# Five sums of weights by transfers that add, issued by GpSimd, in place of VectorE

## The chip, the cores and the metric

One core of one Trainium2 chip runs the kernel. The metric is the device time of one execution in microseconds (us), the median of three runs. The core's engines are PE (TensorE, matrix products), DVE (VectorE), ACT (ScalarE), POOL (GpSimd) and SP (SyncE, which here only issues transfers); 16 DMA engines move the data. Each engine works through its own queue in order, and semaphores order the engines against each other.

## What is computed

For 64 items x of 128 x 1024 there are two stages, each with its residual:

```python
w = weights[conditions]                      # one 128 x 128 matrix per item
x = x + einsum('bct,bcd->bdt', x, w)
H = einsum('btd,od->bto', x, W)              # W is 1024 x 1024, the same for all items
xa = einsum('btd,brd->btr', x, A[adapter_idx])
delta = einsum('btr,bor->bto', xa, Bm[adapter_idx]) * s_b
x = x + H + delta
```

## The kernel before

The kernel moves the second stage ahead of the first: x is multiplied by W plus the identity and by the low-rank adapter, and then the result z by the item's condition matrix plus the identity. Items go in pairs, 32 steps in all. W is cut in 4 x 3 blocks b00 to b32 of 256 rows by 342 columns (a tile of 128 partitions x 2 x 342 numbers, 342 KB). The pair's x is cut in the same manner, and a fast scheme for block products needs, for a pair, 20 products of sums of x blocks with sums of W blocks in place of 24 plain ones. The sums of W are the same for all steps, so they are made once, during step 0.

Step 0 (function `dense`, L1541 to L1557) runs plain 32-bit products on the raw blocks as they arrive from memory. Step 1 (`whole_product`) runs 32-bit products on the sums of W. All later steps (`product`, L1377) run on sums that are split in a high part (ACT, `hi_of`, into `w_hi`) and a rest (DVE, `rest_of`, into `w_lo`). Products and sums share their numbers: the sum "2" is the weight of product 2, and it stands in the slot `slot("lo", "2")` of `w_lo_raw`; an intermediate sum has a letter or an "a" ("f", "12a"). The names "hi" and "lo" of a slot only say in which of two raw tiles it lies.

What sets the order in the first 45 us is written out by hand, a list for each engine:

- SP (L386 to L413): loads x and the 12 blocks of W, then x of step 1, then waits for the split of the adapter matrices B (`z_hi[0]` and `z_lo[0]`, used here as scratch) and stores both parts to the table `b_split` in DRAM (`save_b`), loads the adapter A of step 1, the condition matrices of step 0, waits for both stores (`b_saved` at 32, L412) and loads from that table the rows of step 0 (`load_b`) into `b_stack_raw`.
- POOL (L467 to L505): adds the identity to six blocks of W as they arrive, writes the scaled adapter columns of step 0 (`first_rides`), and after the last block, b22 (L494), picks the scalings of step 1 and makes its adapter columns (`make_rides`, L276 to L299), and writes them beside the sums (L501 and L502, `whole_rides_ready`), which PE needs at product 5 of step 1.
- DVE (L1174 to L1263): the sums, in the order of the blocks' arrival (`DVE_SUMS` lists it; `made` waits for a sum by its place in that list), the sums of x for step 1, the adapter's first product of step 0, then `rest_c` (L1234, the rest of the condition matrices, which waits for ACT's `hi_of_c`), and behind it the last sums: 3, 6, 12a, 12, 1a and 1, and the rests of z.
- ACT (L740 to L834): the high parts in the order 17, 13, 5, 15, then the high part of B, then 2, 0, 4, 14, 18, 10, 7 and 11 (L756 to L772), then `hi_of_c`, the two `turned_xa` (which write `g_sb`), and `take_b` (L776), which makes `b_stack`.
- PE (L1560 to L1596): `dense` of the 12 blocks; ahead of the last, b22, stand the two turns of the adapter's first product and the three products `lora("10")`, `lora("11")`, `lora("12")`, which wait for `g_sb` and for `b_stack` (`b_ready`, L1587). Then step 1 begins with product 17, the adapter products of item 0, products 5 and 15 and a part of the condition product of step 0, then 13 and 2.

## Time and profile before

| | us |
|---|---|
| median of three runs | 772.71 |
| lowest and highest of the three | 772.51, 773.09 |
| the profiled execution | 773.48 |
| its span in the profile | 771.7 |
| PE busy in it | 760.3 (99%) |
| DVE, ACT and POOL busy | 613.8, 503.9, 190.1 |

In the profile, the start is where engines wait for blocks of W, and from 75 us on the steps repeat. The timeline of an engine lists its instructions in order of time, with equal ones merged: the start, the length of the whole group, the count (x3), and in brackets how long the engine had been idle before and what it waited for. PE's records of a 32-bit product count two for each of the kernel's matmuls. A transfer shows on its issuing engine's queue (SPq) only with the time that the issue took; its landing is in the view of its tile.

### The profile page before, as it was taken

To read this page: it belongs to the slowest core of one execution; us is meant where nothing else is said; L and a number is where in the kernel's file an instruction comes from. 1 tells how busy PE (TensorE), PEld (TensorE's weight loads), DVE (VectorE), ACT (ScalarE), POOL (GpSimd) and SP (SyncE) were. 2 spreads that over 40 slices of the span, in tenths; PEclk is the share of its full clock that TensorE was granted. 3 is DMA by queue.
4 is the path that set the end of the run, shared out by engine and by line. 5 is a ranking of instruction groups with operands and counts; after the bars stand their busy time and mean duration, and the time that the engine had idled before them with its cause. 6 is when DMAs were issued, how large, how long until landed. Compare 5 with 4: busy or idle time off the path is not lost.

```text
span 771.7 us, 16748 instructions
## 1 busy us (share of the span) xinstructions
PE 760.3 (99%) x4418; PEld 719.3 (93%) x4418; DVE 613.8 (80%) x1386; ACT 503.9 (65%) x1173; POOL 190.1 (25%) x428
## 2 busy tenths in 40 slices
PE   7999999999999999999999999999999999999998
PEld 4567999999999999999999999999999999999997
DVE  5999977788777788777788777788777788777774
ACT  3476666676666676666676666676666676666673
POOL 2733202233212333202332212323212232212200
PEclk9999999999999999999999999999999999999999
DMA  8433343432343432333432343432343432343222
GB/s 288 169 131 116 124 144 123 151 120 90 122 143 122 150 117 94 122 143 122 150 118 92 122 143 122 150 112 98 122 143 122 150 117 94 122 143 122 89 90 83
DMA packets 47291, 98.32 MB, mean 127 GB/s; under 512 B 6438, under 2 KB 25894, under 8 KB 47270
## 3 DMA queue, kind: packets, MB, share of 16 engines
q1 hardware_dynamic: 47266, 98.08, 37.4%
q8 instruction: 9, 0.15, 0.1%
q14 instruction: 12, 0.10, 0.0%
q10 hardware_dynamic: 4, 0.00, 0.0%
HBM read 63.45 MB, written 34.60 MB: 127 GB/s over the span
## 4 chain that ended last, share of the span: by engine, by line
PE 87%; DVE 3%; DMA 1%; issue 1%; ACT 0%; SPq 0%; DVEq 0%; ACTq 0%
PE bank L1381 73%; PE o_ps L1442 4%; PE bank L1420 3%; PE o_ps L1441 3%; PE o_ps L1443 3%; DMA out<-o_sb 1%; DVE c_sb L892 1%; DVE w_lo L889 1%; DVE z_lo L889 0%; DVE x_lo L889 0%; PE bank L1425 0%; PE o_ps L1432 0%; DVE x_raw L889 0%; ACT x_hi L510 0%; ACT z_hi L510 0%
## 5 line engine op out<-in xcount | busy, mean ns | idle before, releaser
L1381 PE MATMUL bank<-w_hi,x_hi 128*128 128x342 f32 (+2 forms) x1200 | 390.5, 325 | 0.7 <-ACT c_sb L510 0.6
L1381 PE MATMUL bank<-w_lo,x_hi 128*128 128x342 f32 (+2 forms) x1200 | 387.1, 323 | 0.0
L1381 PE MATMUL bank<-w_hi,x_lo 128*128 128x342 f32 (+2 forms) x1200 | 386.5, 322 | 0.0
L1381 PEld LDWEIGHTS bank<-w_hi,x_hi 128*128 128x128 f32 x1200 | 225.8, 188 | 9.8 <-ACT c_sb L510 2.1
L1381 PEld LDWEIGHTS bank<-w_lo,x_hi 128*128 128x128 f32 x1200 | 225.6, 188 | 2.8
L1381 PEld LDWEIGHTS bank<-w_hi,x_lo 128*128 128x128 f32 x1200 | 226.1, 188 | 0.0
L889 DVE TENSOR_TENSOR x_lo<-x_raw,x_hi 128x256 fp32r<-128x256 f32 (+1 forms) x270 | 145.5, 547 | 32.0 <-ACT x_hi L510 27.3
L510 ACT ACTIVATE x_hi<-x_raw 128x256 fp32r<-128x256 f32 (+1 forms) x270 | 133.7, 507 | 52.5 <-PE bank L1381 45.7
L303 POOL TENSOR_TENSOR w_lo<-a_ride,w_hi 128x160 fp32r<-128x160 f32 x30 | 15.6, 519 | 507.0 <-ACT w_hi L510 507.0
L510 ACT ACTIVATE c_sb<-bank 128x342 f32<-128x342 f32 x190 | 85.7, 452 | 41.0 <-PE bank L1381 38.6
L510 ACT ACTIVATE z_hi<-c_sb 128x340 fp32r<-128x340 f32 (+1 forms) x128 | 60.4, 490 | 54.8 <-DVE c_sb L892 54.8
L892 DVE TENSOR_TENSOR c_sb<-bank,c_sb 128x342 f32<-128x342 f32 x186 | 91.1, 504 | 3.6 <-PE bank L1420 2.5
L510 ACT ACTIVATE o_sb<-o_ps 128x512 f32<-128x512 f32 x124 | 73.9, 596 | 14.3 <-PE o_ps L1443 12.6
L889 DVE TENSOR_TENSOR x_lo<-t_sb,x_hi 128x512 fp32r<-128x512 f32 x60 | 41.5, 692 | 36.2 <-ACT x_hi L510 36.2
L889 DVE TENSOR_TENSOR z_lo<-c_sb,z_hi 128x340 fp32r<-128x340 f32 (+1 forms) x128 | 69.4, 544 | 0.4 <-ACT z_hi L510 0.2
L889 DVE TENSOR_TENSOR xa_sum<-bank,c_sb 128x16 f32<-128x16 f32 x31 | 5.4, 174 | 62.7 <-PE bank L1381 62.7
L510 ACT ACTIVATE bank<-bank 128x342 f32<-128x342 f32 (+1 forms) x93 | 41.3, 444 | 15.8 <-PE bank L1381 15.3
L1441 PE MATMUL o_ps<-z_hi,c_hi 128*128 128x512 f32 x126 | 50.5, 401 | 0.0
L1442 PE MATMUL o_ps<-z_lo,c_hi 128*128 128x512 f32 x126 | 49.8, 396 | 0.0
L1443 PE MATMUL o_ps<-z_hi,c_lo 128*128 128x512 f32 x126 | 49.5, 393 | 0.0
L279 POOL TENSOR_TENSOR a_ride<-a_now,s_now 128x32 f32<-128x32 f32 x93 | 43.7, 496 | 16.8 <-DMA a_now<-lora_a 10.1
L1420 PE MATMUL bank<-b_stack,g_sb 128*128 128x340 f32 (+1 forms) x192 | 46.4, 324 | 0.5 <-ACT b_stack L510 0.5
(104 smaller groups left out, 878.2 us busy)
## 6 DMA issues: line engine op xcount, KB each, us to landing
x_raw<-xT SPq DMA_DIRECT2D x62, 512.0 KB, 4.9
out<-o_sb SPq DMA_DIRECT2D x62, 512.0 KB, 2.7
b_stack_raw<-b_split SPq DMA_DIRECT2D x128, 128.0 KB, 2.4
a_now<-lora_a SPq DMA_DIRECT2D x64, 64.0 KB, 3.4
c_raw<-cond_w SPq DMA_DIRECT2D x64, 64.0 KB, 1.8
w_lo_raw<-wB SPq DMA_DIRECT2D x7, 342.0 KB, 7.5
w_hi_raw<-wB SPq DMA_DIRECT2D x5, 342.0 KB, 6.0
x_raw<-xT SPq DMA_DIRECT2D x4, 256.0 KB, 4.7
```

The costliest lines, as they stand in the source:

```text
L279: unit.tensor_tensor(to, a_now[:, n, k:k + count, :], s_now[:, n:n + 1].unsqueeze(2).to_broadcast([P, count, 2 * R]), ALU.mult).then_inc(a ...
L303: unit.tensor_tensor(left_rides(w_lo), rides(0, 5), left_rides(w_hi), ALU.subtract).then_inc(ride_ready, 1)
L510: return nc.scalar.activation(to, x, ACT.Copy)
L889: return nc.vector.tensor_tensor(to, x, y, ALU.subtract)
L892: return nc.vector.tensor_tensor(to, x, y, ALU.add)
L1381: last = nc.tensor.matmul(bank[:, lo:hi], x[:, left, c * C:(c + 1) * C], w[:, c, FIRST[o]:FIRST[o] + WIDTH[o]], start=opens and c == 0 and ...
L1420: nc.tensor.matmul(main_of(bank_of(j, d, role), cols.stop - cols.start), g_sb[n][:, :], b_stack[:, cols], start=False, stop=True, skip_gro ...
L1441: nc.tensor.matmul(bank[:, :], c_hi[:, n, :], z_hi[n][:, cols], start=True, stop=False)
L1442: nc.tensor.matmul(bank[:, :], c_hi[:, n, :], z_lo[n][:, cols], start=False, stop=False)
L1443: nc.tensor.matmul(bank[:, :], c_lo[:, n, :], z_hi[n][:, cols], start=False, stop=True)\
```

## The change

Five sums leave DVE's list: 2, 18, 11, 12 and 1. Each is now one transfer that POOL issues, which adds a block to what its destination holds (`add_on`, with `accum_op`). Before each but the first, POOL waits until the one before has landed (`dma_summed`, 16 for each). The destinations of 2 and 18 are first filled by SP with the blocks b30 and b31, loaded from DRAM a second time, between the loads of x for step 1 and the stores of B; POOL waits for both (`first_parts_landed`). The other three already stand in their slots: "11a" in slot 11, "12a" in block b31's slot and "1a" in b02's. The adds of 2 and 18 stand in POOL's list behind the identity of b22, the one of 11 behind the pick of the scalings and ahead of `make_rides`, the ones of 12 and 1 behind the copies of L501 and L502. `made` waits for `dma_summed` where a reader names one of the five; ACT's list of high parts stays in its order. DVE waits for "f" now ahead of sum 14. Some semaphores are merged (`ident_zero` into `ident_ready`, `ones_ready` and `zeros_ready` into `filled`), which changes no wait's meaning.

```diff
@@ -55,8 +55,10 @@
     DENSE = ("b12", "b01", "b21", "b30", "b20", "b10", "b00", "b11", "b31", "b02", "b32", "b22")
     SPLITS = ("17", "13", "5", "15", "2", "0", "4", "14", "18", "10", "7", "11", "9", "8", "16", "1", "3", "19", "6", "12")
     POOL_SUMS = ("i21a", "i21b", "i10", "i11a", "i11b", "i00", "i32", "i22")
-    DVE_SUMS = ("s", "5", "v", "e", "f", "0", "2", "7", "18", "4", "y", "11a", "14", "10", "11", "3", "6", "12a", "12",
-                "1a", "1", "9", "16a", "16", "19a", "19")
+    DVE_SUMS = ("s", "5", "v", "e", "f", "0", "7", "4", "y", "11a", "14", "10", "3", "6", "12a", "1a", "9", "16a", "16",
+                "19a", "19")
+
+    DMA_SUMS = ("2", "18", "11", "12", "1")

     WHOLE_SUMS = ("u_0", "u12", "v", "u_1", "u", "u910", "u67", "u11", "u54", "u3")

...
@@ -263,6 +265,9 @@
                 eng.wait_ge(pool_summed, max(on_pool))
             if on_dve:
                 eng.wait_ge(dve_summed, max(on_dve))
+            on_dma = [DMA_SUMS.index(n) + 1 for n in names if n in DMA_SUMS]
+            if on_dma:
+                eng.wait_ge(dma_summed, max(on_dma) * 16)

         def left_rides(w):
             return w[:, :, 0:5 * EDGE].rearrange("p c (o q) -> p o c q", q=EDGE)[:, :, :, 0:R]
@@ -401,6 +406,8 @@
             sp.dma_start(cond_sb[:, :], cond_idx).then_inc(cond_landed, 16)
             load_x(0, 0, 1, 0)
             load_x(0, 0, 1, 1)
+            for o, b in (("2", "b30"), ("18", "b31")):
+                sp.dma_start(slot("lo", o), wB[int(b[1]), int(b[2]), :, :, :]).then_inc(first_parts_landed, 16)
             sp.wait_ge(b_hi_ready, 1)
             save_b(0, z_hi[0])
             sp.wait_ge(b_lo_ready, 1)
@@ -464,11 +471,17 @@
                 nc.gpsimd.tensor_tensor(where, where, ident[:, :].unsqueeze(1).to_broadcast([P, 2, P]), ALU.add)\
                     .then_inc(pool_summed, 1)

-            nc.gpsimd.memset(ident[:, :], 0.0).then_inc(ident_zero, 1)
-            pool.wait_ge(ident_zero, 1)
+            def add_on(name, to, x):
+
+                if DMA_SUMS.index(name):
+                    pool.wait_ge(dma_summed, DMA_SUMS.index(name) * 16)
+                nc.gpsimd.dma_start(to, x, accum_op=ALU.add).then_inc(dma_summed, 16)
+
+            nc.gpsimd.memset(ident[:, :], 0.0).then_inc(ident_ready, 1)
+            pool.wait_ge(ident_ready, 1)
             nc.gpsimd.affine_select(out=ident[:, :], in_=ident[:, :], compare_op=ALU.not_equal, fill=1.0,
                                     base=0, pattern=[[-1, P]], channel_multiplier=1).then_inc(ident_ready, 1)
-            pool.wait_ge(ident_ready, 1)
+            pool.wait_ge(ident_ready, 2)
             pool.wait_ge(adapter_landed, 16)
             pool.wait_ge(s_tab_ready, 1)
             pick_scalings(0, 0, 0)
@@ -492,14 +505,24 @@
             add_identities("b32", 84)
             pool.wait_ge(w_landed["b22"], 16)
             add_identity("b22", 1, 0, 44, 84)
+            pool.wait_ge(first_parts_landed, 32)
+            made(pool, "f")
+            add_on("2", slot("lo", "2"), slot("hi", "12"))
+            add_on("18", slot("lo", "18"), slot("hi", "12"))
             pool.wait_ge(first_scaled, 8)
             pick_scalings(0, 0, 1)
+            made(pool, "11a", "e")
+            add_on("11", slot("lo", "11"), slot("hi", "6"))
             make_rides(pool, nc.gpsimd, 0, 0, 1)

             dense_through(pool, "b10")
             pool.wait_ge(a_summed, 4)
             nc.gpsimd.tensor_copy(left_rides(w_lo_raw), rides(0, 5)).then_inc(whole_rides_ready, 1)
             nc.gpsimd.tensor_copy(right_rides(w_lo_raw), rides(5, 4)).then_inc(whole_rides_ready, 1)
+            made(pool, "12a", "s")
+            add_on("12", w_block("b31"), slot("hi", "19"))
+            made(pool, "1a", "i00")
+            add_on("1", w_block("b02"), w_block("b00"))
             pool.wait_ge(whole_rides_ready, 2)
             step(0, 1)
             run_steps(pool, step)
...
@@ -814,7 +837,7 @@
             made(act, "19", "11")
             in_place("6")
             hi_a1(0, 1, 1)
-            made(act, "19a", "14", "18")
+            made(act, "19a", "14", "18", "2")
             in_place("12")
             begin_c02(0, 1)
             turned_xa(0, 1, 0, 1)
@@ -1171,10 +1194,10 @@
             def summed(name):
                 dve.wait_ge(whole_summed, WHOLE_SUMS.index(name) + 1)

-            nc.vector.memset(ones[:, :], 1.0).then_inc(ones_ready, 1)
-            nc.vector.memset(xa_cols[0][:, :], 0.0).then_inc(zeros_ready, 1)
-            nc.vector.memset(xa_cols[1][:, :], 0.0).then_inc(zeros_ready, 1)
-            dve.wait_ge(ident_ready, 1)
+            nc.vector.memset(ones[:, :], 1.0).then_inc(filled, 1)
+            nc.vector.memset(xa_cols[0][:, :], 0.0).then_inc(filled, 1)
+            nc.vector.memset(xa_cols[1][:, :], 0.0).then_inc(filled, 1)
+            dve.wait_ge(ident_ready, 2)
             nc.vector.tensor_copy(ident_r[:, :], ident[:, :]).then_inc(ident_r_ready, 1)
             rest_of("17", w_block("b12"))
             dve.wait_ge(w_landed["b01"], 16)
@@ -1190,14 +1213,10 @@
             add("f", slot("hi", "12"), w_block("b21"), slot("hi", "19"), ALU.subtract)
             made(dve, "e")
             add("0", slot("lo", "0"), slot("hi", "6"), slot("hi", "19"), ALU.subtract)
-            made(dve, "f")
-            add("2", slot("lo", "2"), slot("hi", "12"), w_block("b30"), ALU.add)
             dve.wait_ge(b_hi_ready, 1)
             subtract(z_lo[0][:, :], b_raw[:, :], z_hi[0][:, :]).then_inc(b_lo_ready, 1)
             made(dve, "i10")
             add("7", slot("lo", "7"), w_block("b10"), w_block("b12"), ALU.subtract)
-            dve.wait_ge(w_landed["b31"], 16)
-            add("18", slot("lo", "18"), slot("hi", "12"), w_block("b31"), ALU.add)
             made(dve, "i11b")
             add("4", slot("lo", "4"), w_block("b11"), w_block("b12"), ALU.subtract)
             dve.wait_ge(w_landed["b02"], 16)
@@ -1205,6 +1224,7 @@
             made(dve, "i00")
             add("11a", slot("lo", "11"), w_block("b00"), w_block("b12"), ALU.subtract)
             made(dve, "i32")
+            made(dve, "f")
             add("14", slot("lo", "14"), slot("hi", "12"), w_block("b32"), ALU.add)
             dve.wait_ge(x_landed[1][0], 16)
             dve.wait_ge(x_landed[1][1], 16)
@@ -1217,8 +1237,6 @@
             add("10", slot("lo", "10"), slot("hi", "6"), slot("lo", "8"), ALU.subtract)
             summed("u_1")
             whole("u", subtract, x_whole[:, U, :], x_whole[:, U, :], raw(0, 1)[:, 0, 2, :])
-            made(dve, "11a")
-            add("11", slot("lo", "11"), slot("lo", "11"), slot("hi", "6"), ALU.add)
             summed("u")
             whole("u910", plus, x_whole[:, U9:U, :], twice(x_whole[:, U, :]), x_whole[:, U1:U6, :])
             whole("u67", subtract, x_whole[:, U6:U5, :], twice(raw(0, 1)[:, 0, 2, :]), x_whole[:, U1:U6, :])
@@ -1239,12 +1257,8 @@
             add("6", w_block("b11"), w_block("b11"), w_block("b01"), ALU.subtract)
             dense_through(dve, "b31")
             add("12a", w_block("b31"), w_block("b31"), w_block("b32"), ALU.subtract)
-            made(dve, "12a")
-            add("12", w_block("b31"), w_block("b31"), slot("hi", "19"), ALU.add)
             dense_through(dve, "b02")
             add("1a", w_block("b02"), slot("lo", "8"), w_block("b30"), ALU.subtract)
-            made(dve, "1a")
-            add("1", w_block("b02"), w_block("b02"), w_block("b00"), ALU.add)
             rest_z("10", 0, 0, 0)
             rest_z("11", 0, 0, 0)
             dve.wait_ge(product_done["17"], 1)
...
```

## Rows read from the trace of the kernel before

**Rows 1.** The page's busy times: engine, us (share of the span), instructions.

```profile
PE 760.3 (99%) x4418; PEld 719.3 (93%) x4418; DVE 613.8 (80%) x1386; ACT 503.9 (65%) x1173; POOL 190.1 (25%) x428
```

**Rows 2.** Windows: stretch, length, busy times by engine, granted clock, DMA share, GB/s.

```profile
17.00:22.50 5.50, 4.74 (x16) 2.76 (x15) 4.29 (x4) 2.05 (x3) 4.83 (x7) 1.00 1.06 395
22.50:27.50 5.00, 4.71 (x16) 2.77 (x15) 4.38 (x9) 2.21 (x3) 3.80 (x6) 1.00 0.60 237
...
250.00:500.00 250.00, 250.00 (x1515) 244.21 (x1514) 199.29 (x464) 170.01 (x402) 62.77 (x143) 1.00 0.38 127
```

**Rows 3.** Timeline of PE, 0 to 75 us: start, length, what, idle before.

```profile
20.68 2.67 PE L1553 MATMUL bank<-w_lo_raw,x_raw 128*128 128x358 f32 x8 [0.76 <-POOL w_lo_raw L451]
23.64 2.67 PE L1553 MATMUL bank<-w_hi_raw,x_raw 128*128 128x358 f32 x8 [0.29 <-POOL w_hi_raw L451]
...
36.21 0.71 PE L1420 MATMUL bank<-b_stack,g_sb 128*128 128x342 f32 x3 [0.47 <-ACT b_stack L510]
...
40.67 2.52 PE L1397 MATMUL bank<-w_lo_raw,x_whole 128*128 128x358 f32 x8
42.77 0.65 PE L1441 MATMUL o_ps<-z_hi,c_hi 128*128 128x512 f32 x1
...
70.04 0.43 PE L1381 MATMUL bank<-w_hi,x_hi 128*128 128x342 f32 x1 [0.63 <-ACT c_sb L510]
```

**Rows 4.** Timeline of ACT, 0 to 75 us.

```profile
17.63 1.42 ACT L510 ACTIVATE w_hi<-w_lo_raw 128x684 fp32r<-128x684 f32 x2
...
28.34 2.10 ACT L510 ACTIVATE w_hi<-w_lo_raw 128x684 fp32r<-128x684 f32 x3 [0.95 <-DVE w_lo_raw L1152]
31.77 0.42 ACT L510 ACTIVATE c_hi<-c_raw 128x256 fp32r<-128x256 f32 x1 [1.33 <-DVE c_raw L892]
33.31 0.28 ACT L510 ACTIVATE g_sb<-o_ps 128x128 fp32r<-128x128 f32 x1 [1.13 <-PE o_ps L1432]
...
35.01 1.06 ACT L510 ACTIVATE b_stack<-b_stack_raw 128x1024 fp32r<-128x1024 f32 x1 [1.25 <-DMA b_stack_raw<-b_split]
```

**Rows 5.** Timeline of SP, 0 to 75 us; its lengths are those of the issues.

```profile
15.74 0.84 SPq L318 DMA_DIRECT2D x_raw<-xT  x2
17.75 0.74 SPq L378 DMA_DIRECT2D b_split<-z_hi  x1
...
30.92 2.16 SPq L338 DMA_DIRECT2D b_stack_raw<-b_split  x4
```

**Rows 6.** Waits of SP's queue, 0 to 80 us: total, times, longest.

```profile
SPq L323 <- DMA b_split<-z_lo: 1.2, 1, 1.2
```

**Rows 7.** Timeline of POOL, 0 to 75 us.

```profile
24.86 0.33 POOL L457 TENSOR_TENSOR w_lo_raw<-w_lo_raw,ident 128x84 f32<-128x84 f32 x1
...
30.19 1.26 POOL L279 TENSOR_TENSOR a_ride<-a_now,s_now 128x32 f32<-128x32 f32 x3 [3.90 <-DMA a_now<-lora_a]
...
36.14 0.93 POOL L502 COPY w_lo_raw<-a_ride 128x128 f32<-128x128 f32 x1
```

**Rows 8.** Views of the tiles w_lo_raw (342 KB) and c_raw (64 KB): issue to landing.

```profile
DMA to landing us min/median/max: 4.3/7.5/8.0
...
DMA to landing us min/median/max: 1.7/2.0/2.4
```

**Rows 9.** Timeline of DVE, 0 to 75 us.

```profile
14.83 1.64 DVE L1152 TENSOR_TENSOR w_lo_raw<-w_hi_raw 128x684 f32<-128x684 f32 x2
...
32.41 0.56 DVE L889 TENSOR_TENSOR c_lo<-c_raw,c_hi 128x256 fp32r<-128x256 f32 x1
...
36.05 2.65 DVE L1152 TENSOR_TENSOR w_lo_raw<-w_lo_raw,w_hi_raw 128x684 f32<-128x684 f32 x3
...
40.41 0.87 DVE L1152 TENSOR_TENSOR w_lo_raw<-w_lo_raw 128x684 f32<-128x684 f32 x1 [0.86 <-PE bank L1397]
```

**Rows 10.** Groups of PE by shape, 4 to 12 us: count, busy us, mean ns, idle.

```profile
L1553 PE MATMUL bank<-w_lo_raw,x_raw 128*128 128x342 f32 x8 | 4.9, 795 | 1.6 <-DMA w_lo_raw<-wB 1.6
L1553 PE MATMUL bank<-w_hi_raw,x_raw 128*128 128x342 f32 x6 | 1.9, 454 | 0.0
```

More of the change, by code:

```diff
@@ L128, in cond_resid_kernel @@
         x_half_landed = [sem(f"x_half_landed{n}") for n in range(2)]
-        ones_ready = sem("ones_ready")
+        filled = sem("filled")
         s_spread = sem("s_spread")
@@ L140, in cond_resid_kernel @@
         table_loaded = sem("table_loaded")
-        ident_zero = sem("ident_zero")
         ident_ready = sem("ident_ready")
         ident_r_ready = sem("ident_r_ready")
-        zeros_ready = sem("zeros_ready")
         pool_summed = sem("pool_summed")
         dve_summed = sem("dve_summed")
+        dma_summed = sem("dma_summed")
+        first_parts_landed = sem("first_parts_landed")
         w_hi_ready = sem("w_hi_ready")
@@ L741, in _ @@
             act.dma_start(s_row[:, :], scalings).then_inc(s_landed, 16)
-            act.wait_ge(ident_ready, 1)
+            act.wait_ge(ident_ready, 2)
             copy(table[0:32, 0:1], ident[0:32, 0:1]).then_inc(table_loaded, 1)
@@ L1560, in _ @@
             pe.wait_ge(s_landed, 16)
-            pe.wait_ge(ones_ready, 1)
+            pe.wait_ge(filled, 1)
             nc.tensor.matmul(o_ps[0][:, 0:NAD], ones[0:1, :], s_row[0:1, :], start=True, stop=True).then_inc(s_spread, 1)
```

## The prediction

> **What bounds the kernel now.** I read the page first. PE is busy in 760.3 of 771.7 us and DVE in 80% [rows 1]; between 250 and 500 us PE is busy for all of the 250.00 [rows 2]. Nothing that this change touches runs there, and what PE loses in the first 75 us is not given back later: PE has no gap in which to catch up. The question is only by how much the change moves PE's start-up.
>
> The second view was PE's timeline of that start. After its first block PE waits four times: 0.76 and 0.29 us for columns that POOL writes, 0.47 us at 36.21 for `b_stack`, the first operand of the adapter products, and 0.63 us at 70.04 for a copy by ACT [rows 3]. Together that is 2.15 us, the most that any relief of DVE could bring. None of the four names DVE. DVE even ends its list of sums early: it waits 0.86 us for PE ahead of 40.41 [rows 9].
>
> The third view was the list of ACT, because the adapter products at 36.21 wait for two things that ACT makes: `g_sb` (33.31) and `b_stack` (35.01) [rows 4]. ACT's list is in order, and the high parts of 2, 18 and 11 stand in it ahead of both. The fourth was SP's queue: `b_stack` waits for transfers that SP issues from 30.92 on, after a wait for the store of B [rows 5, 6].
>
> **What it removes.** Five DVE instructions of about 0.88 us (three in 2.65 us) [rows 9], 4.4 us. The adds of 2 and 18 stood where DVE waited for blocks and for POOL anyway. The one of 11 stood ahead of `first_split`, which leads to `g_sb`, but PE reaches the turn behind its own dense products, and after it `b_stack` is what is late, by its transfer [rows 3, 4]. The ones of 12 and 1 stood just before the 0.86 us wait for PE [rows 9]; a wait takes their place. Value of the removal: 0, at most 2.15 us as above.
>
> **The two added loads.** SP issues two more transfers between the loads of x, whose issue ends at 16.58 (15.74 + 0.84), and the store of the high part of B at 17.75, for which it had been waiting [rows 5]. At about 0.6 us each (0.84 us for two of x is the nearest row) they fill that gap; the issue costs nothing. Their data does cost. From 17 to 22.5 us the DMA engines are full (share 1.06, 395 GB/s), and then run at 237 GB/s with a share of 0.60 until 27.5 [rows 2]; I read the first as the loads and the second as mostly the two stores of B, which stand behind the loads in SP's queue. Two blocks of 342 KB are 0.70 MB; at 395 GB/s that is 1.8 us, by which the stores end later. SP waits for them (1.2 us of wait in before, so there is no slack [rows 6]), issues the loads of B 1.8 us later, and `b_stack` starts at 36.8 in place of 35.01, PE's adapter products at 38.0 in place of 36.21. That alone is +1.8 us. It would be 0 if the loads fitted beside the stores in the 40% that those leave idle, and more if POOL's adds, which fall in the same stretch, take share from the stores; I take 1.8, with bounds 0 and 2.8.
>
> **The three adds ahead of the adapter products.** POOL ends the identity of b22 at 25.2 (24.86 + 0.33) [rows 7]. The filled slots of 2 and 18 end with the loads at about 24.3 (22.5 + 1.8), and with the time that a small transfer takes to report I put the start of the first add at 25.7. Then the three adds run one behind the other, since POOL waits for each landing before it issues the next. The trace has no transfer by POOL, none that adds, and none between two tiles of SBUF. The nearest rows: 64 KB in an idle queue take 1.7 us at least, 342 KB in a full queue take 4.3 to 8.0 us [rows 8]. These are my two ends, 1.7 and 8.0 for each add. I take 4.3: same size, a queue only half full, but one that has to read the destination as well as the source. So 2 lands at 30.0, 18 at 34.3 and 11 at 38.6.
>
> ACT waits for 2 at about 17.6, where it started on it in before [rows 4]. At 30.0 it does 2, 0, 4 and 14, at 34.3 it does 18, 10 and 7, and at 38.6 it does 11. Behind it are 0.70 us for the high part (2.10 for three), 0.42 for `c_hi`, two times 0.28 for `g_sb` and 1.06 for `b_stack` [rows 4], 2.7 us in all and 2.6 with their overlap. The B rows have landed by then (36.8). PE's adapter products start at 41.2 in place of 36.21, **+5.0 us**. The 1.8 us of the loads are inside this, not on top: the later of the two sets the start.
>
> What is queued behind these waits. On ACT: the condition matrices' high part, `g_sb`, `b_stack` and all the copies of z. On DVE: `rest_c` waits for ACT's `c_hi`, so DVE stands from about 31 to 39.2, and the sums 3, 6, 12a and 1a and the rests of z come after it. In before `c_lo` ran 3.8 us ahead of the adapter products (32.41) [rows 9], now 2.0 ahead; but two adds of 0.88 us are gone behind it, so the rests of z end as far ahead of the condition products (42.77 in before [rows 3]) as they did. On POOL: `make_rides` starts behind the issue of add 11, about 35.3 (1 us for the issue, above the 0.6 of SP) in place of 30.19, takes the same 6.9 us until its copies end (37.07 in before [rows 7]), and is done at 42.3; PE needs it at 40.67 + 5.0 = 45.7 [rows 3]. The add of 12 then waits for 12a (about 43.3), lands at 47.6, the one of 1 at 51.9; ACT needs it about 57. Those two I cost at 0; their cover is 5 us.
>
> **The sum.** The profiled execution took 773.5 us against a median of 772.7; the sum made on it is carried to the median as a difference. 772.7 + 5.0 = 777.7.
>
> A rule of the skill against this length. The Trainium skill, "DMA: Bandwidth & Descriptors", section "Anatomy of one DMA", gives a transfer issued by GpSimd about 2.0 us plus its bytes at 436 GB/s, which would be an estimate of 2.8 us for each add; no row here shows such a transfer. By that the third add would land at 34.1, ACT would be through at 36.7, and the loads (38.0) would set the start: the time of the first rival below, not mine.
>
> **The rivals.**
> *Short adds.* Below 3.3 us each, the third lands before 35.6 and ACT is through before 38.2; then the late `b_stack` sets the start, +1.8 to +2.8 us, 774.5 to 775.5. For it: the DMA engines are nearly idle from 28 us on. Against: each add is a chain of issue, read, read, write and report, and the smallest 342 KB row is 4.3 us. 0.16.
>
> *The chain, and a slow clock after it.* PE idles 0.47 + 5.0 us in one stretch. At the start of the kernel, after such idle time, eight 32-bit matmuls took 795 ns each, while later ones of the same shape took 454 [rows 10]: the shorter is that of 2.4 GHz, the longer nearer 1.2 GHz, though the granted clock in the windows reads 1.00. If PE falls back, the next eight cost (795 - 454) x 8, 2.7 us as busy times overlap little, about 2.3 from their starts: 777.7 + 2.3 = 780.0. The Trainium skill, "TensorE: Matmul & The Clock Gate" (section "HAM oscillation"), says that waits between bursts of matmuls put the clock back to half; here no wait of such length shows between PE's first block and the end. 0.20.
>
> *Long adds.* Above 5.3 us each (a destination read that halves the rate, or an issue on POOL of over 1 us), +8 to +16 us, 780.7 to 789. 0.08.
>
> *Not slower.* DVE's relief decides, and the adds are hidden: if they land by 33 us (2.4 us each) and the two loads fit beside the stores, ACT is never late. Then DVE's 4.4 us can take away the 0.63 us at 70.04 and some of POOL's 0.76 and 0.29, where POOL works beside DVE: 772.7 - 0.6 = 772.1, at the most 770.6. Against: both conditions at once, and DVE's wait of 0.86 us for PE swallows what it saves. 0.06. That the transfers do not replace the DVE work is excluded by the lists.
>
> **How the numbers follow.** The forecast, adds of 3.3 to 5.3 us, +2.0 to +8.0, 774.7 to 780.7: 0.50. The range has to leave out no more than 0.2: 774.3 to 782.5 leaves out most of the long adds, the not-slower case and the tail of the clock case. A difference of about 0.2% (1.5 us) is what a measurement of this kernel can tell from none. Faster by more: 0.02. Within: 0.06 (the rest of the not-slower case, and the low edge of the short adds). Slower: 0.92.
>
> **What would show it.** In the profile of the changed kernel: the first `w_hi` copy after `z_hi` on ACT at 30 and the one of 11 at 38.6, POOL as what ACT waited for, or a DMA; the adapter products of PE at 41.2 with an idle time of about 5.5 us named `b_stack` or `g_sb`; `b_stack_raw` loaded by 36.8; DVE with a gap of some 7 us ahead of `c_lo`; from 75 us on the same steps. The prediction is wrong if ACT reaches `c_hi` before 35, if PE waits anywhere else for over 1 us, or if the span outside the first 75 us changes.

## The result, and the profile after

The changed kernel takes 785.05 us (median of four runs, 784.82 to 785.59), the kernel before, run beside it, 772.87 us: a ratio of 1.0155, 95% interval 1.0143 to 1.0168. It is slower by 12.2 us. The prediction said 777.7 us, 774.3 to 782.5. Its sign holds, and so does the path it named (adds one after another, ACT's list behind them, PE last); its size does not, and a second cost, PE's slow clock, was missing from its sum.

| | before | after |
|---|---|---|
| profiled execution, us | 773.48 | 785.16 |
| span in the profile, us | 771.7 | 783.3 |
| PE starts the adapter products of step 0 | 36.21 | 45.01 |
| PE starts product 5 of step 1 | 40.67 | 52.33 |
| PE busy, 250 to 500 us | 250.00 | 250.00 |

The lines on the span and on product 5 close the sum: product 5 starts 11.66 us late, and the span is 11.6 us longer, so the loss is complete by 53 us. (The medians differ by 12.2 us and the two profiled executions by 11.7: the profiled one of before lies 0.6 us above its median.)

The page's line of busy times (engine, us, share of the span, instructions), which answers [rows 1]. PE's work has grown by 2.3 us though it does the same 4418 instructions; DVE has five fewer, POOL five more.

```profile
PE 762.6 (97%) x4418; PEld 721.1 (92%) x4418; DVE 609.1 (78%) x1381; ACT 503.7 (64%) x1173; POOL 194.2 (25%) x433
```

PE's largest wait (engine, line, what it waited for: us in total, times, longest). In before this wait was 0.47 us.

```profile
PE bank L1434 <- ACT b_stack L533: 9.7, 1, 9.7
```

PE's timeline around it (start, length, what, count, idle before), which answers [rows 3].

```profile
32.79 2.51 PE L1567 MATMUL bank<-w_lo_raw,x_raw 128*128 128x342 f32 x8
45.01 1.19 PE L1434 MATMUL bank<-b_stack,g_sb 128*128 128x342 f32 x3 [9.70 <-ACT b_stack L533]
46.00 4.76 PE L1567 MATMUL bank<-w_lo_raw,x_raw 128*128 128x342 f32 x8
50.55 1.47 PE L1411 MATMUL bank<-w_lo_raw,x_whole 128*128 128x342 f32 x4
51.60 0.89 PE L1434 MATMUL bank<-b_stack,g_sb 128*128 128x342 f32 x3
52.33 2.52 PE L1411 MATMUL bank<-w_lo_raw,x_whole 128*128 128x358 f32 x8
```

Read two things here. The wait ends 8.80 us later than in before (45.01 against 36.21). And behind it eight matmuls of one shape take 4.76 us, where the same eight took 2.51 us before the wait, at 32.79. From the adapter products to product 5 there are 7.32 us, in before 4.46 (40.67 - 36.21). That is 2.86 us more for the same work: 8.80 + 2.86 = 11.66.

The windows say what that is (stretch, length, busy times of PE, PEld, DVE, ACT, POOL with counts, granted clock, DMA share, GB/s). The clock is at 0.50, which is the level of 1.2 GHz, from 42 us on, and goes back to full within the window from 50 on.

```profile
40.00:42.00 2.00, 0.00 (x0) 0.00 (x0) 0.00 (x0) 0.00 (x0) 1.77 (x7) 0.65 1.08 175
42.00:44.00 2.00, 0.00 (x0) 0.00 (x0) 0.38 (x2) 1.49 (x5) 0.59 (x3) 0.50 0.01 4
...
45.00:50.50 5.50, 5.49 (x11) 3.69 (x12) 3.35 (x6) 1.55 (x4) 1.20 (x1) 0.50 0.39 58
...
50.00:55.00 5.00, 5.00 (x19) 3.49 (x18) 2.94 (x6) 3.39 (x9) 2.02 (x3) 0.91 0.79 259
250.00:500.00 250.00, 250.00 (x1515) 244.24 (x1515) 199.07 (x464) 168.85 (x400) 59.48 (x136) 1.00 0.38 125
```

Why the wait is so long is in ACT's list, which answers [rows 4].

```profile
33.09 2.76 ACT L533 ACTIVATE w_hi<-w_lo_raw 128x684 fp32r<-128x684 f32 x4 [15.86 <-DMA w_lo_raw<-w_hi_raw]
37.74 2.10 ACT L533 ACTIVATE w_hi<-w_lo_raw 128x684 fp32r<-128x684 f32 x3 [1.89 <-DMA w_lo_raw<-w_hi_raw]
42.51 0.77 ACT L533 ACTIVATE w_hi<-w_lo_raw 128x684 fp32r<-128x684 f32 x1 [2.67 <-issue]
43.19 0.40 ACT L533 ACTIVATE c_hi<-c_raw 128x256 fp32r<-128x256 f32 x1
43.49 0.26 ACT L533 ACTIVATE g_sb<-o_ps 128x128 fp32r<-128x128 f32 x1
43.65 0.27 ACT L533 ACTIVATE g_sb<-bank 128x128 fp32r<-128x128 f32 x1
43.81 1.05 ACT L533 ACTIVATE b_stack<-b_stack_raw 128x1024 fp32r<-128x1024 f32 x1
```

The three groups start at the landings of 2, 18 and 11, and behind the last stands the tail to `b_stack`. The wait of 15.86 us is for the first add. The 2.67 us ahead of the third group are labelled "issue", since the profile didn't pair them with a transfer, but POOL's list does (second column is the issue alone, it answers [rows 7]):

```profile
26.36 1.33 POOL L478 DMA_DIRECT2D w_lo_raw<-w_hi_raw  x1 [2.30 <-DMA w_lo_raw<-wB]
33.37 1.20 POOL L478 DMA_DIRECT2D w_lo_raw<-w_hi_raw  x1 [5.67 <-DMA w_lo_raw<-w_hi_raw]
...
38.24 1.19 POOL L478 DMA_DIRECT2D w_lo_raw<-w_hi_raw  x1 [3.38 <-DMA w_lo_raw<-w_hi_raw]
...
47.02 1.20 POOL L478 DMA_DIRECT2D w_lo_raw<-w_hi_raw  x1 [3.93 <-DVE w_lo_raw L1175]
52.98 1.19 POOL L478 DMA_DIRECT2D w_lo_raw<-w_hi_raw  x1 [4.76 <-DVE w_lo_raw L1175]
```

The second and the third follow on the landing of the one before; the first waited for SP's second loads of b30 and b31. The view of the tile w_lo_raw, from 24 to 45 us, has the time from issue to landing of these three: the first took 6.7 us, the third 4.2.

```profile
DMA to landing us min/median/max: 4.2/4.3/6.7
```

What ran beside the first is in SP's queue, whose line answers [rows 5]: SP issues the loads of `b_stack_raw` when both stores of B have landed, at 31.79, and in before at 30.92. So the stores were under way for most of the first add, and behind them in SP's list stand the small loads of the adapter and the condition matrices (24.79 and 27.20). From 26 to 31 us the DMA engines moved 243 GB/s at a share of 0.83, in before 125 GB/s at 0.37.

```profile
31.79 2.20 SPq L343 DMA_DIRECT2D b_stack_raw<-b_split  x4
```

### The profile page after: what moved, and what is told of

Its sections match the earlier page's. It is cut to its first block, busy times and chain, and to the rows that moved or that the text cites. A ratio compares the mean times of both kernels' runs of the same rounds, so it can differ in the third digit from the quotient of the medians.

```text
span 783.3 us, 16759 instructions
## 1 busy us (share of the span) xinstructions
PE 762.6 (97%) x4418; PEld 721.1 (92%) x4418; DVE 609.1 (78%) x1381; ACT 503.7 (64%) x1173; POOL 194.2 (25%) x433
## 3 DMA queue, kind: packets, MB, share of 16 engines
q0 software_dynamic: 1360, 1.75, 1.4%
## 4 chain that ended last, share of the span: by engine, by line
PE 86%; DVE 3%; DMA 1%; issue 1%; ACT 0%; SPq 0%; DVEq 0%; ACTq 0%
PE bank L1395 71%; PE o_ps L1456 3%; PE bank L1434 3%; PE o_ps L1455 3%; PE o_ps L1457 3%; DMA out<-o_sb 1%; DVE c_sb L915 1%; DVE w_lo L912 1%; DVE z_lo L912 0%; DVE x_lo L912 0%; PE bank L1439 0%; PE o_ps L1446 0%; DVE x_raw L912 0%; ACT x_hi L533 0%; ACT z_hi L533 0%
## 5 line engine op out<-in xcount | busy, mean ns | idle before, releaser
L533 ACT ACTIVATE c_sb<-bank 128x342 f32<-128x342 f32 x190 | 85.7, 451 | 43.8 <-PE bank L1395 38.6
```

Of the source, the lines that this page charges most:

```text
L533: return nc.scalar.activation(to, x, ACT.Copy)
```

## The experiments

The clock's cost is read everywhere in the same way: the time from the start of the adapter products to that of product 5 less the 4.46 us of before. I call it the second leg, and the start of the adapter products less 36.21 the first leg.

### Is DVE's relief worth anything, and do the late adds cost anything?

Only 12 and 1 are done by transfers, with the waits of the change; 2, 18 and 11 stay with DVE. Against the changed kernel:

```diff
-    DMA_SUMS = ("2", "18", "11", "12", "1")
+    DMA_SUMS = ("12", "1")
...
+            add("2", slot("lo", "2"), slot("hi", "12"), w_block("b30"), ALU.add)
...
```

> Only the sums 12 and 1 are added by transfers; 2, 18 and 11 stay with DVE and nothing is loaded twice. Theory of the ordered chain (only adds that stand ahead of ACT's operands of the adapter products cost anything): the same as before, 772.9 within 0.5 us, the adapter products at 36.2. Rival, that every such transfer costs in itself (POOL's time, traffic, DVE beside it): a fifth or more of the loss for each, 775 to 777.

Measured: 773.32 us, ratio 1.0002 (0.9992 to 1.0011), adapter products at 35.67, 0.5 us earlier than in the profiled execution of before (the blocks of W came earlier in this one, see the end). No difference that can be measured: two of the five transfers with DVE's relief by those two sums are worth nothing together.

### What do the two loads cost by themselves?

The kernel before, with two loads of the same size at the same place in SP's queue, into tiles that are idle there (`o_sb`, and `b_stack_raw`, whose later load waits for it).

```diff
+            for n, to, b in ((0, o_sb, "b30"), (1, b_stack_raw, "b31")):
+                sp.dma_start(to[:, 0:2 * N].rearrange("p (c q) -> p c q", q=N), wB[int(b[1]), int(b[2]), :, :, :])\
+                  .then_inc(extra_landed[n], 16)
             sp.wait_ge(b_hi_ready, 1)
             save_b(0, z_hi[0])
```

> The kernel before, and the two blocks are loaded a second time at the same place of SP's queue into tiles that are idle; no adds by transfers. By the step of the prediction the stores of B end 1.8 us later: 774.7. By the trace of the changed kernel, where SP issued the loads of B at 31.79 against 30.92: +0.9, 773.7. Rival, that the traffic made the loss: above 780.

Measured: 776.87 us, ratio 1.0043 (1.0029 to 1.0057). Its timeline of PE:

```profile
32.99 2.51 PE L1558 MATMUL bank<-w_lo_raw,x_raw 128*128 128x342 f32 x8
37.99 0.94 PE L1425 MATMUL bank<-b_stack,g_sb 128*128 128x342 f32 x3 [2.48 <-ACT b_stack L514]
38.73 3.94 PE L1558 MATMUL bank<-w_lo_raw,x_raw 128*128 128x342 f32 x8
```

The first leg is 1.78 us, as the prediction worked out (SP issues the loads of `b_stack_raw` at 32.40 in place of 30.92). The second leg, 1.68 us, was in no theory of this run: its window from 38 to 42 us has a granted clock of 0.57. A wait of 2.48 us was enough to lose the full clock. To show that the second leg is the clock and not something that the loads do, the next kernel adds four products of no use (into `o_ps[0]`, overwritten later) where PE would wait:

```diff
+            for n in range(4):
+                nc.tensor.matmul(o_ps[0][:, 0:N], x_raw[0][:, n % 2, 0, 0:C], w_block("b12")[:, n % 2, :],
+                                 start=True, stop=True)
```

> The kernel with the two added loads alone, and PE runs four idle products while it waits for b_stack. The start of the adapter products stays at 38.0. Theory of the slow clock: with the wait of 2.5 us nearly filled, the products after it keep 0.45 us each and 1.7 us come back, 775.1 against 776.9. Rival, that the extra comes from something else: 776.9.

Measured: 774.99 us (eleven runs), ratio 1.0024 (1.0015 to 1.0033). Its timeline of PE, in which L1592 is the filling:

```profile
35.48 2.46 PE L1592 MATMUL o_ps<-w_lo_raw,x_raw 128*128 128x342 f32 x8
37.83 0.71 PE L1425 MATMUL bank<-b_stack,g_sb 128*128 128x342 f32 x3
38.38 2.46 PE L1558 MATMUL bank<-w_lo_raw,x_raw 128*128 128x342 f32 x8
```

The adapter products start as late as without the filling, the matmuls behind them take 2.46 us again, and the kernel is 1.9 us faster. So the loads cost 1.7 to 1.8 us by delay (774.99 against 773.25 beside it, and the first leg), and 1.9 us by the clock that the delay loses.

### How much of the change is the clock?

The changed kernel with sixteen such products at the same place.

```diff
+            for n in range(16):
+                nc.tensor.matmul(o_ps[0][:, 0:N], x_raw[0][:, n % 2, 0, 0:C], w_block("b12")[:, n % 2, :],
+                                 start=True, stop=True)
```

> The changed kernel, and PE runs 16 idle products into a bank nobody reads while it waits for b_stack; nothing else is changed. Theory of the slow clock: the wait ends where it did (45.0), but the products after it take 0.45 us in place of 0.9, and 2.9 us come back: 782.2. Rival, that the slow products after the wait have another cause (operands that come late): 785.0, or more if the idle products outlast the wait.

Measured: 784.52 us, ratio 1.0145, but in two groups: 783.18 and 783.75, 785.30 and 786.21. The profile is of 785.30:

```profile
35.12 9.36 PE L1601 MATMUL o_ps<-w_lo_raw,x_raw 128*128 128x342 f32 x32
45.38 0.71 PE L1434 MATMUL bank<-b_stack,g_sb 128*128 128x342 f32 x3 [0.90 <-ACT b_stack L533]
45.93 2.46 PE L1567 MATMUL bank<-w_lo_raw,x_raw 128*128 128x342 f32 x8
...
49.86 2.52 PE L1411 MATMUL bank<-w_lo_raw,x_whole 128*128 128x358 f32 x8
...
101.87 0.30 PE L1439 MATMUL bank<-ident_r,xa_cols 128*128 128x128 f32 x1 [2.04 <-DVE xa_cols L912]
```

The second leg is gone (49.86 - 45.38 = 4.48). But at 101.87 PE waits 2.04 us, and the clock falls there (0.79 in the window from 100 to 108), so what was saved is lost again. ACT waits 3.08 us for the store of the outputs just before that, at 97.21. Since two of the four runs were 2.3 us faster, I ran the same kernel again to see one of the other group:

> The changed kernel with the 16 idle products once more, with more runs: four runs before lay at 783.2 to 786.2. Theory, that the filled wait keeps the clock, and that the clock can fall later, at another wait of about 2 us in step 3 (for the store of o_sb behind the loads of x): two groups of runs, at 782 to 784 where the mean clock is 1.0 and at 785 to 786 where it is 0.998 or less. Rival, that filling brings nothing: one group at 785.

Measured: 782.95, 782.74, 783.53 and 786.25. This time the profiled run is a fast one, 782.95: adapter products at 45.50, product 5 at 49.97, granted clock 1.00 in every window read, and no later wait of PE over 0.62 us. ACT waits 1.64 us for the same store here, and PE 0.59 us: each 1.4 us less than in the slow one, so PE's later wait goes back to that store. Against 785.05 that is 2.1 us, somewhat less than the 2.86 us of the second leg, in part because the adapter products start 0.5 us later. Why the store lands later in some runs of this kernel is open. Of these eight runs five lie at 782.7 to 783.8 us and three at 785.3 to 786.3.

### How long is an add, and why?

*Transport or the adding?* All five transfers copy in place of adding. The five sums then lack what their slots held, a part of each.

```diff
-                nc.gpsimd.dma_start(to, x, accum_op=ALU.add).then_inc(dma_summed, 16)
+                nc.gpsimd.dma_start(to, x).then_inc(dma_summed, 16)
```

> The changed kernel with the five transfers as plain copies: they overwrite the destination in place of adding to it, so the five sums lack one part. Bytes, order and waits are the same. Theory, that reading the destination and adding is a large part of the 4.6 us from issue to landing: 3.3 us each, the adapter products at about 41, 781. Rival, that a transfer issued by GpSimd takes as long in any case: 785.

Measured: 782.35 us, ratio 1.0111 (1.0095 to 1.0126), adapter products at 43.03. POOL's list, and the tile's view from 24 to 45 us:

```profile
26.37 0.88 POOL L478 DMA_DIRECT2D w_lo_raw<-w_hi_raw  x1 [2.37 <-DMA w_lo_raw<-wB]
32.49 0.73 POOL L478 DMA_DIRECT2D w_lo_raw<-w_hi_raw  x1 [5.24 <-DMA w_lo_raw<-w_hi_raw]
...
37.67 0.72 POOL L478 DMA_DIRECT2D w_lo_raw<-w_hi_raw  x1 [3.63 <-DMA w_lo_raw<-w_hi_raw]
...
DMA to landing us min/median/max: 2.8/4.6/5.8
```

The third alone, in its own window, is the 2.8. A copy of 342 KB takes 2.8 us with the DMA engines otherwise empty, the add in the same place 4.2 us, and its issue holds POOL for 1.20 us in place of 0.72. So adding costs 1.4 us in an empty queue. Only the third place compares like with like: the second copy took 4.6 us, no less than the second add (4.3), since SP issued the loads of `b_stack_raw` beside it at 32.60. The DMA queues of the first 80 us (packets, MB, share of the time of 16 engines), after first and then the copy, say where: more packets for the same sums, and twice the engines' time.

```profile
q0 software_dynamic: 1360, 1.75, 13.8%
...
q0 software_dynamic: 560, 1.75, 6.2%
```

*Does the first add pay for the stores of B?* SP stores B only after the add of 2 has landed; this takes the stores out of its way and puts them in that of the second. SP's list being in order, the small loads behind the stores move too, so that SP issues nothing beside the first add (from 17.67 to 31.07).

```diff
             sp.wait_ge(b_hi_ready, 1)
+            sp.wait_ge(dma_summed, 16)
             save_b(0, z_hi[0])
```

> The changed kernel, but SP stores B only after the add of 2 has landed, so nothing but the small loads runs beside that add. A look at one number: when the add that was issued at 26 lands. Theory, that its 7.1 us against 4.3 of the third came from the stores of B beside it: about 30.4, 4.4 us. Rival, that the first transfer of GpSimd's queue is slow in itself (its first issue took 1.33 us against 1.2): 33 again. The second add will be slower, beside the stores; the whole time is no measure here, 783 to 788.

Measured: 791.86 us, a single run. The first add is issued at 26.70 and takes 4.3 us to land, not the 6.7 of the change (the expectation's 7.1 is about the time to the next issue). The second, which now has the stores beside it, takes until 42.59, from 31.35:

```profile
31.07 2.76 ACT L534 ACTIVATE w_hi<-w_lo_raw 128x684 fp32r<-128x684 f32 x4 [13.52 <-DMA w_lo_raw<-w_hi_raw]
42.59 2.10 ACT L534 ACTIVATE w_hi<-w_lo_raw 128x684 fp32r<-128x684 f32 x3 [8.76 <-DMA w_lo_raw<-w_hi_raw]
```

So it isn't being the first in POOL's queue that makes an add slow. An add of this size costs 4.2 to 4.3 us with the DMA engines to itself, 6.7 us beside the end of the stores and the small loads, and 11.2 us beside the whole of the stores. How much of the 2.4 us between the first two is the stores' and how much the small loads' isn't shown.

*Does the chain of the three matter?* The three are issued one behind the other without a wait, and each reader waits for all of them. The last two lose their wait for each other in the same way.

```diff
-                if DMA_SUMS.index(name):
-                    pool.wait_ge(dma_summed, DMA_SUMS.index(name) * 16)
-                nc.gpsimd.dma_start(to, x, accum_op=ALU.add).then_inc(dma_summed, 16)
+                nc.gpsimd.dma_start(to, x, accum_op=ALU.add).then_inc(dma_summed[DMA_SUMS.index(name) > 2], 16)
```

> The changed kernel, but GpSimd issues the adds of 2, 18 and 11 without waiting for one another, on one semaphore, and readers wait until all three have landed; ACT's order is that of the changed kernel. Theory of the chain (each add is mostly latency: issue and report): all three land by about 35, ACT is through at about 43, and the adapter products start at 43 in place of 45, 782 to 783.5. Rival, that an add is mostly data (342 KB that take their 4 us of the DMA engines): the three land no earlier than 40, and then ACT does eight high parts behind them, 785 to 790.

Measured: 784.43 us, ratio 1.0145, above the 782 to 783.5 of the theory, and not by the rival's way either. All three land by 37.5 us (theory 35, rival 40 or later), 5.0 us before the third add of the change, yet PE gains 0.36 us. First the line of ACT:

```profile
37.52 5.41 ACT L529 ACTIVATE w_hi<-w_lo_raw 128x684 fp32r<-128x684 f32 x8 [20.56 <-DMA w_lo_raw<-w_hi_raw]
```

and that of PE:

```profile
44.65 1.19 PE L1430 MATMUL bank<-b_stack,g_sb 128*128 128x342 f32 x3 [9.62 <-ACT b_stack L529]
```

ACT now has all eight high parts still to do, 5.4 us, because the first of them waits for the last landing. In the change it does seven of them between the landings. The transport was shortened and ACT's own work took its place.

### Can it be mended?

*Order of ACT alone.* The high part of 2 moves behind the split of z, those of 18 and 11 behind the first seed of step 1, where their first readers are still far. Nothing that leads to `b_stack` waits for a transfer by POOL any more.

```diff
             hi_of("17", w_block("b12"))
...
-            made(act, "2")
-            in_place("2")
...
-            made(act, "18")
-            in_place("18")
...
-            made(act, "11", "e")
-            dense_through(act, "b20")
-            in_place("11")
...
+            made(act, "2")
+            in_place("2")
...
+            made(act, "18", "11", "e")
+            in_place("18")
+            in_place("11")
```

> The changed kernel with ACT's high parts of 2, 18 and 11 taken from ahead of the operands of the adapter products and put where ACT stands idle in step 1, before DVE needs them; all five transfers and both loads stay. Theory of ACT's order: b_stack is then late by its transfer alone, the adapter products start at about 37.2, 773.5 to 774.5. Rival, that the adds and loads themselves hold the start back: still above 778.

Measured: 779.24 us, ratio 1.0079 (1.0062 to 1.0096). It takes away 5.8 of the 12.2 us, less than expected. Its timeline of PE:

```profile
37.65 0.72 PE L1433 MATMUL bank<-b_stack,g_sb 128*128 128x342 f32 x3 [2.18 <-ACT b_stack L534]
38.21 4.15 PE L1566 MATMUL bank<-w_lo_raw,x_raw 128*128 128x342 f32 x8
...
59.29 1.42 PE L1410 MATMUL bank<-w_lo_raw,x_whole 128*128 128x342 f32 x4 [0.91 <-ACT c_sb L534]
```

and one line of ACT's:

```profile
57.46 1.44 ACT L534 ACTIVATE w_hi<-w_lo_raw 128x684 fp32r<-128x684 f32 x2 [3.05 <-DMA w_lo_raw<-w_hi_raw]
```

The first leg falls from 8.80 to 1.44 us with the five adds and both loads still in place, so ACT's order is what carries the adds to PE. The wait of 2.18 us still loses the clock (second leg 1.71 us). The rest, some 2 us, is new: the adds of 12 and 1, free in the first experiment, are late here. The one of 12, issued at 43.57 beside the loads of x (223 GB/s from 45 to 50 us), takes 7.8 us; POOL issues the one of 1 behind it, at 51.94, and ACT waits for that one until 57.46. This last reading rests on the trace of this kernel alone.

*All of it.* ACT's order is that of the last kernel, but with the high part of 2 still later (behind those of 9 and 8), the two loads stand behind the stores of B, and there is no chain, neither among the first three nor between the last two. The lines on the loads:

```diff
-            for o, b in (("2", "b30"), ("18", "b31")):
-                sp.dma_start(slot("lo", o), wB[int(b[1]), int(b[2]), :, :, :]).then_inc(first_parts_landed, 16)
             sp.wait_ge(b_hi_ready, 1)
             save_b(0, z_hi[0])
...
+            for o, b in (("2", "b30"), ("18", "b31")):
+                sp.dma_start(slot("lo", o), wB[int(b[1]), int(b[2]), :, :, :]).then_inc(first_parts_landed, 16)
```

> The five sums by transfers, with the three causes taken away: the second loads stand behind the stores of B, the adds of 2, 18 and 11 do not wait for one another, and ACT makes their high parts in step 1. If the three causes are all, the adapter products start at 36 to 37 and the time is that of before or up to 1.5 us above it, 773 to 774.5. Rival, that the adds' traffic beside the loads of B and of x holds something else back: 776 or more, with a wait on a transfer to show for it.

Measured: 774.98 us (ten runs, 773.05 to 778.31), ratio 1.0023 (1.0008 to 1.0038). Three runs with a mean granted clock of 0.998 took 777.0 to 777.2, six others 773.05 to 775.53. The profile is of one of the three: adapter products at 36.91 after 1.98 us of wait, product 5 at 43.07, a second leg of 1.70 us. In this kernel the clock falls in some runs and not in others; how long PE waited in the others isn't known, as only this one was profiled. With three products to fill the wait:

> The five sums by transfers with the three causes taken away, and PE runs three idle products in the 2 us that it still waits for b_stack. Theory, that the upper of its runs (777, mean clock 0.998) were the clock and the lower (773.1 to 774.4) the rest: all runs at 773.0 to 774.5, no group at 777. Rival, that the transfers' traffic spreads the times by itself: again up to 777 or more.

Measured: 773.93 us (eleven runs), ratio 1.0013 (1.0004 to 1.0022), ten of them between 773.57 and 774.70. In its timeline most of the loss is gone: a first leg of 0.26 and a second of 0.20 us.

```profile
36.47 0.90 PE L1429 MATMUL bank<-b_stack,g_sb 128*128 128x342 f32 x3
37.21 2.46 PE L1562 MATMUL bank<-w_lo_raw,x_raw 128*128 128x342 f32 x8
```

One run of each of the two kernels (778.31 and 776.82) was long at a full clock; I have no profile of either, and what they waited for is open. No version with the five transfers is faster than the kernel before.

## Why the prediction was wrong in size and right in kind

Two steps of it failed. It had the clock at nothing in the sum, and the clock cost 2.86 us. And it had each add at 4.3 us, where the first took 6.7 us, so that with smaller terms the third landed 3.9 us late.

- **What bounds the kernel.** Right. PE is again busy for the whole of 250 to 500 us, and all of the loss is ahead of product 5.
- **The removal, worth 0.** Nothing contradicts it. For 12 and 1 the first experiment measures removal and transfers together, and finds nothing. For 2, 18 and 11 no run has the removal without the cost; the nearest is the mended and filled kernel, which has all five removed and is not faster than before.
- **The two loads, 1.8 us by bytes over the measured rate.** Right to 0.1 us by itself: forecast 38.0, measured 37.99. What was missed is that this delay alone loses the clock, for another 1.7 to 1.9 us. So the "short adds" rival would not have given 774.5 to 775.5 but the 776.9 of the kernel with the loads alone.
- **The start of the first add.** Forecast 25.7, measured 26.36, as the two loads landed later than I had put them: +0.66 us.
- **The length of an add, 4.3 us each: the term that failed in the first leg.** Forecast landings 30.0, 34.3 and 38.6; measured 33.1, 37.7 and 42.5. For the second and third, with at most the small loads of `b_stack_raw` beside them, 4.3 was right (33.37 to 37.74 and 38.24 to 42.51). The first took 6.7, +2.4 us. I had read the DMA engines as half free from 22.5 to 27.5 [rows 2], and nearly idle from 28 on, and had not asked what stood there after the change, though my own step had moved the end of the stores back by 1.8 us. The kernel in which the stores wait gives 4.3 us for this same add, so the 2.4 us come from what SP's list has beside it: the stores, and the small loads behind them. Missing too was the step from one landing to the next issue, 0.28 us (33.09 to 33.37) and 0.50 us (37.74 to 38.24, behind the pick of the scalings). The sum is 0.66 + 2.4 + 0.28 + 0.50, but for rounding the 3.9 us by which the third landing is late.
- **ACT's tail, 2.6 us.** Right: 45.01 - 42.51 = 2.50. First leg forecast +5.0, measured +8.80: the 3.9 us less 0.1.
- **The clock: the term that was missing.** The mechanism stood as a rival with its price, 2.3 us; it measured 2.86 us. The price was for the eight matmuls behind the wait, and they took 2.25 us more from start to start (46.00 to 50.55, in before 36.76 to 39.06); left out were the adapter products themselves (0.44) and the matmuls behind the eight (0.17). The failure is in how the numbers followed: I made "the chain and a slow clock" exclusive of the forecast and gave it 0.20. The forecast itself had PE idle for 5.5 us, and the row from 4 to 12 us [rows 10] shows matmuls of 795 ns after idle time; behind the wait of the change the same shape took 777 ns, where the granted clock reads 0.50. Had the clock been a term of the sum, not a rival, the forecast would have been 780.0; with the adds at the upper end of that case (+8.0) 783.0. That is still 2 us short: the first leg of 8.80 lay just inside what I had kept for long adds. The Trainium skill, "TensorE: Matmul & The Clock Gate" (section "HAM oscillation"), states the fall to half when matmuls wait between bursts; the trace agrees, with 0.50 granted from 42 us on.
- **Long adds.** Of the three only the first was above the 5.3 us from which I counted an add as long, yet the sum passed that rival's +8. Long adds and a slow clock came together. By setting each against the forecast one by one I left their sum outside the range.
- **The queues behind the waits.** Right: the copies of the adapter columns end at 43.1 and don't delay product 5, DVE's gap ahead of `c_lo` is 9.6 us (forecast 7), and PE has no wait behind product 5 that would be the adds' of 12 and 1.
- **The rule on length.** The Trainium skill, "DMA: Bandwidth & Descriptors", section "Anatomy of one DMA", gave an estimate of 2.8 us. The plain copy measures that in an empty queue; the adding transfer does not, 4.2 us, and the measurement decides. Nor would adds of a copy's length have saved the kernel: the copying one still has its adapter products at 43.03, since its first copy takes 5.8 us beside the stores.
- **The signs of being wrong.** None of the three came: ACT reached `c_hi` at 43.19, PE had no other new wait of over 1 us, and the span changed only in its first 53 us. They watched the path, which held; none watched the granted clock, where a fall below 1.00 behind the wait would have shown the missing term.

## What to carry to other kernels

Ask of an operation that is moved to a transfer not how long it takes but who stands in line behind its landing: here two of five were free, and three cost 12 us because one engine's fixed order had them ahead of an operand of PE. Length is to be worked out beside what shares the DMA engines at that moment, each landing of a chain anew, and not with the rate of the stretch before. And where a step of the sum makes PE idle for some microseconds behind full work (here 1.98 us were enough in the profiled run), the slow clock belongs in the sum itself, with its price from rows at either level, and not among the rivals.

## What the hardware showed that I had not expected

- Idle times of 2.0 to 2.5 us ended in a lower clock, in this place: 2.48 us in the profiled run of the loads alone (granted clock 0.57 from 38 to 42 us; four of its five runs have a mean clock of 0.998), 2.18 us in the one profile of its kernel (0.57 from 38 to 42), 1.98 us in the one profile of the mended kernel (0.58), and 2.04 us further on in a filled one (0.79 from 100 to 108). After waits of 0.47 to 1.02 us at the same place the windows read 1.00. The price, by the second leg, was 1.7 us after the three short waits, and 2.86, 2.69, 2.17 and 2.01 us after waits of 9.70, 7.77, 9.62 and 15.93 us (the change, the copies, no chain, the stores that wait): it doesn't grow with the wait once this is long.
- Filling such a wait with products of no use wins it back (776.87 to 774.99 us), as long as no later wait does the same.
- Five transfers that add need 1360 packets where five copies need 560, and take 2.2 times the engines' time (13.8% against 6.2%); one takes 1.4 us more in an empty queue, and 0.5 us more of POOL.
- POOL and DVE get in each other's way. POOL's add of the identity to b00, the first row below (b32 has its own at 23.55, which takes 1.35 and 0.72 us likewise), starts at 20.59 in before, 0.17 us behind a sum of DVE (20.42 to 21.35), and takes 1.35 us; after the change POOL starts first, at 20.71, and takes 0.72 us, and it is DVE's sum of 20.86 that takes 1.30 us in place of some 0.9. In these rows the one that starts second pays. In all four profiled kernels that keep 2 and 18 with DVE this add takes 1.35 us, in the nine that don't 0.72 or 0.73. The rows of before:

```profile
20.59 1.35 POOL L464 TENSOR_TENSOR w_hi_raw<-w_hi_raw,ident 128x256 f32<-128x256 f32 x1
20.42 0.93 DVE L1152 TENSOR_TENSOR w_lo_raw<-w_hi_raw,w_lo_raw 128x684 f32<-128x684 f32 x1 [0.45 <-DMA w_lo_raw<-wB]
```

and those of after:

```profile
20.71 0.72 POOL L471 TENSOR_TENSOR w_hi_raw<-w_hi_raw,ident 128x256 f32<-128x256 f32 x1
20.86 1.30 DVE L1175 TENSOR_TENSOR w_lo_raw<-w_lo_raw 128x684 f32<-128x684 f32 x1 [0.21 <-DMA w_lo_raw<-wB]
```

- PE gains nothing by that. It reaches its wait at 35.31, 0.4 us earlier than in before, but the blocks of W came earlier in that execution: POOL's group of identities that waits for b10 starts at 17.16 against 17.67. From there to PE's wait it is 18.15 us after and 18.07 us before; in the first experiment, whose lists are those of before up to there, the group starts at 16.84 and PE's wait at 34.91, again 18.07 us. Differences of half a microsecond in when a stretch begins are those of one execution against another, and belong to no edit.
